# The last unit's ninth step sums the second buffer, and ScalarE centres the next batch's tokens: a fused attention and FFN kernel on one core

## The reference

```python
xn = layernorm(layernorm(x)) * g1 + b1         # queries: twice normalised
cn = layernorm(context) * g2 + b2
q, k, v = xn @ Wq.T, cn @ Wk.T, cn @ Wv.T      # 16 heads of 32
s = where(mask, q @ k.T / sqrt(32), -inf)      # [16 heads, 1024, 2048]
x1 = x + (softmax(s) @ v) @ Wo.T + bo
xd, wd = mx_fp6(layernorm(x1)), mx_fp6(W)      # blocks of 32 share a scale
out = x1 + xd @ wd.T + bias
```

## Time and profile before

| | |
|---|---|
| Median of 3 runs | 4500.66 us (4495.67 to 4505.8) |
| The profiled execution's own time | 4507.71 us |
| Its span | 4505.9 us |
| PE busy | 4345.9 us (96%) |
| DVE busy | 3443.6 us (76%) |
| ACT busy | 2814.4 us (62%) |
| POOL busy | 2718.9 us (60%) |
| Mean granted TensorE clock | 0.993 |
| Queue q0 (merges) | 318.79 MB, 35.3% of 16 engines' span |
| Queue q1 (loads and stores of SP) | 207.83 MB, 15.0% |

### The profile page before, as it was taken

One profiled execution on the slowest core, in us unless ns is written; L12 is line 12 of the kernel. 1 busy time (PEld: TensorE's weight loads), 2 busy tenths in 40 slices (PEclk: granted clock), 3 DMA queues, 4 the chain that ended last, 5 costly groups with the idle time before them and its releaser, 6 DMA issues.

```text
span 4505.9 us, 89640 instructions
## 1 busy us (share of the span) xinstructions
PE 4345.9 (96%) x36880; PEld 1506.5 (33%) x36880; DVE 3443.6 (76%) x4023; ACT 2814.4 (62%) x5128; POOL 2718.9 (60%) x1706
## 2 busy tenths in 40 slices
PE   4999999999999999999999999999999999999999
PEld 2322343223432234322343223422234222342223
DVE  5788667886678866888668886688866888668885
ACT  3387734877447864478645785458754587546784
POOL 2288552885428854388544885348853588525884
PEclk9999999999999999999999999999999999999999
DMA  5355642557326573356633556335663365543654
GB/s 191 73 118 118 150 136 61 120 118 180 109 59 123 114 192 99 68 117 121 177 100 69 119 120 175 102 77 116 123 167 106 75 123 115 167 111 74 123 113 108
DMA packets 190012, 532.35 MB, mean 118 GB/s; under 512 B 28625, under 2 KB 102673, under 8 KB 148386
## 3 DMA queue, kind: packets, MB, share of 16 engines
q0 software_dynamic: 43776, 318.79, 35.3%
q1 hardware_dynamic: 145826, 207.83, 15.0%
HBM read 110.98 MB, written 21.01 MB: 29 GB/s over the span
## 4 chain that ended last, share of the span: by engine, by line
PE 73%; DVE 12%; DMA 5%; ACT 4%; issue 3%; POOL 2%; SPq 0%; DVEq 0%; ACTq 0%; POOLq 0%
PE banks L1048 20%; PE banks L1060 17%; PE banks L956 16%; PE banks L1016 12%; PE banks L1091 5%; DVE max_parts L621 5%; DMA wdT<-wkT_wvT_wqT 3%; ACT region L835 2%; PE banks L925 2%; DMA sums<-wkT_wvT_wqT 2%; PE banks L950 1%; DVE amax L569 1%; DVE x_stats L536 1%; DVE region L759 1%; DVE qscale L571 1%
## 5 line engine op out<-in xcount | busy, mean ns | idle before, releaser
L621 DVE TENSOR_REDUCE max_parts<-banks 128x2 f32<-128x1024 f32 x2048 | 2402.1, 1218 | 454.3 <-PE banks L1016 442.4
L835 ACT ACTIVATE region<-banks 128x512 f32<-128x512 f32 x4096 | 2191.1, 616 | 506.2 <-PE banks L1048 401.1
L427 POOL TENSOR_TENSOR wkT_wvT_wqT<-region 128x1024 f32<-128x1024 f32 x528 | 1284.7, 2518 | 668.0 <-ACT region L835 662.6
L1048 PE MATMUL banks<-queries_stacked,keys_stacked 98*32 98x512 f16 x16384 | 1317.7, 384 | 21.6 <-ACT values L822 7.1
L1060 PE MATMUL banks<-region,values 128*32 128x512 f32 x8192 | 1076.8, 600 | 12.3 <-ACT region L835 9.2
L1048 PEld LDWEIGHTS banks<-queries_stacked,keys_stacked 98*32 98x32 f16 x16384 | 415.5, 95 | 1149.3 <-ACT region L835 842.0
L1016 PE MATMUL banks<-keys_stacked,queries_stacked 33*128 33x512 f16 x4096 | 701.5, 386 | 7.2 <-DVE max_parts L621 3.5
L956 PE MATMUL banks<-region,wkT_wvT_wqT 128*128 128x512 f16 x2304 | 557.3, 381 | 12.6 <-DMA wkT_wvT_wqT<-weights_split 10.3
L427 POOL TENSOR_TENSOR sums<-region 128x1024 f32<-128x1024 f32 x144 | 358.8, 2617 | 92.1 <-ACT region L835 91.8
L956 PE MATMUL banks<-wkT_wvT_wqT,region 128*128 128x512 f16 x1536 | 368.8, 380 | 0.0
L1016 PEld LDWEIGHTS banks<-keys_stacked,queries_stacked 33*128 33x128 f16 x4096 | 180.2, 93 | 559.4 <-issue 352.2
(11 more groups left out here) (92 smaller groups left out, 3224.0 us busy)
## 6 DMA issues: line engine op xcount, KB each, us to landing
wdT<-wkT_wvT_wqT POOLq DMA_DIRECT2D x96, 1024.0 KB, 11.7
wkT_wvT_wqT<-wkT_wvT_wqT POOLq DMA_DIRECT2D x80, 1024.0 KB, 7.3
sums<-wkT_wvT_wqT POOLq DMA_DIRECT2D x72, 1024.0 KB, 7.3
wkT_wvT_wqT<-sums POOLq DMA_DIRECT2D x40, 1024.0 KB, 7.2
region<-in_x SPq DMA_DIRECT2D x24, 1024.0 KB, 8.9
wkT_wvT_wqT<-weights_split SPq DMA_DIRECT2D x8, 3072.0 KB, 19.0
keys_stacked<-region SPq DMA_DIRECT2D x384, 64.0 KB, 2.0
keys_stacked<-sums SPq DMA_DIRECT2D x384, 64.0 KB, 2.0
```

What stands on the lines that cost most here:

```text
L427: e.tensor_tensor(SUMS[dst][:, half], PR[i][:, half], PR[i + 1][:, half], ALU.add).then_inc(s_pr, 1)
L621: e.tensor_reduce(mpart[:, buf, :, a, t, c], MXB[parity], AX.X, ALU.max).then_inc(s_mxd, 1)
L835: e.activation(PR[u % 4][:, j * HALF:j * HALF + HALF], score_bank(m % NU, kt, j)[0], ACT.Exp, scale=SCALE).then_inc(s_ex, 1)
L1048: mm = e.matmul(dst[HD * t:HD * t + HD, :], KA[0:STR, ds(ka + (j * C + (u + 1) * P + HD * t), HD)], QA[0:STR, ds(qa[j], HALF)], start=True ...
```

## The change

Five things are changed.

1. In unit 7, PE sums the second buffer of unit 6 in the ninth step (t = 8) and not in the sixth (t = 5). ACT copies the bank LB after it, in the tenth tile instead of the seventh.
2. In unit 7, DVE puts pair 4 and the adds of tiles 10 to 13 into the buffer one instead of second. That buffer is free once the unit's first merge has landed, and DVE waits for this. Pair 4 now comes ahead of the inverse of unit 6, and the wait for six steps of PE falls away.
3. SP loads the FFN weights right after the ninth step, ahead of the halves of x.
4. The centring of the next batch's query tokens goes from DVE to ACT, with a new shift made by POOL (`next_rstd`, three small instructions instead of one): chunk 0 at ACT's i = 4 and 5, two 128 x 512 activations each, and chunk 1, four of them, after ACT's last stage.
5. DVE takes chunk 1's statistics at i = 9, all at once, and not at i = 5 and 6.

```diff
-    NEXT_AT = (2, 6)
+    NEXT_AT = (2, T // P - 1)
...
+                e.wait_ge(s_pv, b * (NU * KT) + (NU - 1) * KT + 9 + 4)
+                e.dma_start(SUMS[4], wd_dram).then_inc(s_fl, 16)
...
                 e.wait_ge(s_pv, b * (NU * KT) + NU * KT + 4)
-                e.dma_start(SUMS[4], wd_dram).then_inc(s_fl, 16)
...
+                def next_rstd(c):
+                    e.wait_ge(s_ve, call_next(b, NEXT_AT[c]))
+                    e.wait_ge(s_nx, (b + 1) * NCH + c)
+                    e.tensor_tensor(rs[:, :], ve[:, :], mhalf[:, :], ALU.pow).then_inc(s_nr, 1)
+                    e.wait_ge(s_nr, 2 * (b * XCH + c) + 1)
+                    e.tensor_tensor(nb[:, :], mv[:, :, 0], rs[:, :], ALU.mult).then_inc(s_nr, 1)
+                    e.wait_ge(s_nr, 2 * (b * XCH + c) + 2)
+                    e.tensor_scalar(nb[:, :], nb[:, :], -1.0, None, ALU.mult).then_inc(s_rs, 1)
...
-                    if i in NEXT_AT and b + 1 < B:
-                        rstd(call_next(b, i))
+                    if i == NEXT_AT[0] and b + 1 < B:
+                        next_rstd(0)
                 if b + 1 < B:
-                    low_tokens(b + 1, 0, TF_FIRST)
+                    low_tokens(b + 1, 0, TF_FIRST, halfway=lambda: next_rstd(1))
...
-                                ins = e.tensor_tensor(SUMS[second][:, half], SUMS[second][:, half], PR[t % 4][:, half],
+                                ins = e.tensor_tensor(SUMS[one][:, half], SUMS[one][:, half], PR[t % 4][:, half],
...
                         pair(3, three)
+                        e.wait_ge(s_acc, (3 * m + 1) * 16)
+                        pair(4, one)
                         invert_first(m - 1)
                         invert_rest()
                         normalise(m - 1, n - 1)
-                        e.wait_ge(s_pv, m * KT + 4 + 6)
-                        pair(4, second)
...
-                parts = queries_tokens(b + 1, [call_next(b, i) for i in NEXT_AT]) if b + 1 < B else iter(())
+                parts = [token_stats(c, b + 1, call_next(b, NEXT_AT[c])) if b + 1 < B else iter(()) for c in range(XCH)]
...
+                    if i == TT + 1:
+                        for _ in parts[1]:
+                            pass
                     if i >= 3:
                         y_tile(i - 3)
-                    if i >= 1:
-                        next(parts, None)
+                    if 1 <= i <= NEXT_AT[0]:
+                        next(parts[0], None)
...
+                def centred(c, first, n):
+                    e.wait_ge(s_rs, call_next(b, NEXT_AT[c]))
+                    for i in range(first, first + n):
+                        ins = e.activation(chunk_tokens(c)[:, i, :], chunk_tokens(c)[:, i, :], ACT.Identity,
+                                           bias=nb[:, i:i + 1], scale=rs[:, i:i + 1])
...
-                            if kt == 7 and n > 0:
+                            if kt == 7 and 0 < n < NU - 1:
                                 halfway = lambda: row_sums(m - 1, KT + 6)
+                            if kt == 10 and end:
+                                halfway = lambda: row_sums(m - 1, KT + 9)
...
+                    if i in (4, 5) and b + 1 < B:
+                        centred(0, (i - 4) * 2, 2)
...
+                if b + 1 < B:
+                    centred(1, 0, 4)
...
+                    closing = 8 if end else 5
...
-                                if t == 5:
+                                if t == closing:
                                     sums = [(SUMS[4], (s_ac2, 16 * (b * (2 * NU - 2) + 2 * (2 * g + q))))]
```

More of the change, by code:

```diff
@@ L152, in build @@
             for n, w in (("mean_var", 2), ("var_eps", 1), ("rstd", 1), ("minus_mean_rstd", 1)))
+        nb = sb("minus_mean_rstd", [P, 4], F32)
         mhalf = sb("minus_half", [P, 4], F32)
@@ L208, in build @@
         s_rs = sem("rstd_ready")
+        s_nr = sem("next_rstd_made")
         s_nx = sem("tokens_normalised")
@@ L405, in _, with low_tokens @@
             for b in range(0, B):
-                def low_tokens(b, c, full, call=None):
+                def next_rstd(c):
[6 more added lines that the diff above has]
+                    e.tensor_scalar(nb[:, :], nb[:, :], -1.0, None, ALU.mult).then_inc(s_rs, 1)
+                def low_tokens(b, c, full, call=None, halfway=None):
                     for cc in range(CC):
@@ L412, in low_tokens @@
                             rstd(call)
+                        if cc == 1 and halfway:
+                            halfway()
                 if b == 0:
@@ L551, in centre, with token_stats @@
                 return e.tensor_scalar(dst, src, mean, rstd, ALU.subtract, ALU.mult)
+            def token_stats(c, b, call):
+                e.wait_ge(s_x[c % 3], b * (NCH // 3 * 16) + c // 3 * 16 + 16)
+                if c >= XCH:
+                    e.wait_ge(s_rs, call - 1)
+                yield from norm_stats([chunk_tokens(c)[:, i, :] for i in range(4)], stats, mv, ve[:, :], c < XCH)
             def norm(c, b, call):
@@ L555, in norm @@
                 twice = c < XCH
-                e.wait_ge(s_x[c % 3], b * (NCH // 3 * 16) + c // 3 * 16 + 16)
-                yield from norm_stats(tiles, stats, mv, ve[:, :], twice)
+                yield from token_stats(c, b, call)
                 yield
@@ L812, in turned @@
                                          scale=affine[:, 2 * x_side, cc:cc + 1]).then_inc(done, 1)
+                def centred(c, first, n):
[3 more added lines that the diff above has]
+                                           bias=nb[:, i:i + 1], scale=rs[:, i:i + 1])
+                    if first + n == 4:
+                        ins.then_inc(s_nx, 1)
                 def high_part(f, i, j):
@@ L1133, in quad @@
                                     sums = [(SUMS[buffers(2 * g + q - 1)[0]], (s_acc, 48 * m))]
-                                if t == 5:
+                                if t == closing:
                                     sums = [(SUMS[4], (s_ac2, 16 * (b * (2 * NU - 2) + 2 * (2 * g + q))))]
-                            step(m, n, ex, ka, qa, v, u, t + 1, rows[u], sums=sums, closing=t == 5,
+                            step(m, n, ex, ka, qa, v, u, t + 1, rows[u], sums=sums, closing=t == closing,
                                  between=(lambda: turn_next(ex)) if t == 9 and not end else None)
@@ L1153, in unit @@
                     if end:
-                        left = [(PR[3], None), (second, (s_pr, m * 14 + 16)), (first, (s_acc, 48 * (m + 1)))]
+                        left = [(PR[3], None), (one, (s_pr, m * 14 + 16)), (first, (s_acc, 48 * (m + 1)))]
                     else:
```

## The result

The changed kernel takes 4521.55 us, median of 10 runs (4515.26 to 4526.68), beside 4505.41 us of the kernel before, 10 runs too (4495.67 to 4509.35). The ratio is 1.0039, 95% interval 1.003 to 1.0048. It is slower by about 17 us, outside the range 4484 to 4514, and near the 4522 of the rival *Slower*. The prediction was put on the median of three runs of the kernel before, 4500.66; with ten runs that median is 4505.41, so 4.8 us of the distance to 4500 come from the starting point and some 17 from the sum.

What follows compares the result with a forecast made beforehand. PE was busy nearly all the time, with waits for `wdT` (11.2 us) and a chain of three merges in unit 7. Unit -6.8, load +9.6, clock +10.4, last stage -13.0 gave +0.2 us: 4500 us, range 4484 to 4514.

Steps and rivals of the forecast that it cites:

- Slower: Rival, chance 0.23: the merge waits for all of the load, 2.6 us, and the clock falls every batch; +21.8 us, 4522.
- The wait for the second buffer: Unit 7: PE's wait for `wdT` goes, but the third merge limits the gain to 0.85 us a batch, 6.8 in all.
- DVE's new order: Unit 7: DVE's later pair 4, inverse and adds stay hidden, PE ready 1.3 us ahead of the third merge; cost nothing.
- The load: FFN weights' load between second and third merge in unit 7: costs 1.2 us a batch, +9.6; bounds 0 and 2.6 us.
- The clock: PE's wait before unit 7's last sum lowers the clock in half of the batches: 4 x 2.6 = +10.4 us, bounds 0 and 20.8.
- The last stage: Batches one to seven: first to eighth tile takes the eighth batch's 45.4 us; -13.0 us over seven batches.
- The likeliest case: The wait only moves to PE's last sum, and the last stage pays for load and clock: 4500 us, chance 0.42.
- The clock holds: Rival, chance 0.15: the load costs 1.2 us, but PE's idle time is spread by other waits; -10.2 us, 4490.
- The load slips in: Rival, chance 0.20: the merge takes its turn, 0.3 us a batch, and the clock falls once; -14.8 us, 4486.

Runs made afterwards that it cites:

- the late load: Changed kernel with the FFN weights loaded at their old place, after the halves of x: 4481.73 us, ratio 0.9943 to the kernel before; repeated, 4481.9 us, 0.9932.
- the sooner half of x: Changed kernel with the FFN weights loaded at their old place and the first half of x issued as soon as tile 12 is added: 4484.93 us.
- The fill: Changed kernel with four unread products on PE ahead of its wait for the third merge in unit 7: 4508.19 us, ratio 1.0003 to the kernel before.
- the centring alone: Kernel before with only the centring moved to ACT and the late statistics, unit 7 and FFN weights' load as before: 4495.64 us, ratio 0.9974.
- the load two steps later: Changed kernel with the early load of the FFN weights issued two steps later: 4495.66 us, ratio 0.9975 to the kernel before.
- unit 7 alone: Kernel before with only the change in unit 7, centring left on DVE, FFN weights loaded at their old place: 4499.86 us, ratio 0.9991.
- half the load early: Changed kernel with half of the FFN weights (0.5 MB) loaded early, the other half at the old place: 4498.33 us, one run.

## Why the prediction was wrong, point by point

**The wait for the second buffer** went away as forecast, and its gain was cut by the third merge as forecast. Without the early load unit 7 is 7.8 and 8.4 us shorter in the two profiles with the late load (295.0 against 287.2 and 286.6), for a forecast of 6.8. That this is so close is partly luck: the sum had the last sum 31.0 us after that of first and the first tile 5.0 later, and the profile has 30.1 and 5.8. The merges are quicker than forecast (7.9 and 7.4 us, not 8.3 and 8.2), and x comes later against them, which the forecast had at nothing, or 0.5 us if the merge ends early.

**DVE's new order** was put at nothing. No step of PE in unit 7 waits for DVE, before the last sum or at it. ACT makes PE wait 0.4 to 1.1 us in most batches, 24 to 26 us after the sum of first; in the changed kernel this is hidden by the merge, as forecast. In the kernel with the late load PE has no wait for the merge in four of eight batches, and there it is no longer hidden.

**The load** is the step that failed. The mechanism was named, that the load stands ahead of the merge in a chain without slack, but the term of 1.2 us a batch was far too small. The second to third merge takes 2.75 us more with the early load than without (10.65 against 7.90), which is a little over the upper bound of 2.6; against the kernel before (8.34) it takes 2.3 more. Two things were wrong in how the term was worked out. The rate was taken from a stretch with many loads in flight, 2.6 us for 1 MB; this load takes 3.9 to 6.4 us, 5.0 in the mean. And the cost was taken to be the overlap of two stretches of time, but the merge also moves its own data more slowly behind the load. In the third batch the second to third merge takes 12.25 us, and 8.14 in the same batch with the late load: 4.1 us for this load alone. The load also costs at the third merge: it comes so late that the halves of x are queued behind it before its data is through, and it takes 8.3 us to PE's last sum and not the 7.4 of the kernel with the late load. The run with the sooner half of x shows the same from the other side, 8.0. The prediction had this in its 8.2, so it is no part of the miss. Against the late load the last sum is 3.5 us later in each batch, 28 us, where the prediction priced the load at 9.6. Against the prediction's own sum, which had 32.2 us with the load, it is 33.6: 1.15 us from the second merge, and 0.1 each from its issue and from the third.

**The clock** was taken to fall in half of the batches, 10.4 us. It fell in seven of eight, after waits of 4.1 us in the mean and not 2.5; in the fifth batch it held after 2.64. The first tile came 7.0 us after the last sum and not 5.0, which is 16.3 us over eight batches. The fill shows the clock's price by itself, 13 to 16 us. The clock's miss follows from the load's. Together the two make the unit 2.1 us a batch longer than forecast, 17 us, and with 1.3 us elsewhere that is nearly the whole way from the forecast +0.2 to the measured 18.9.

**The last stage** gave 13.0 us in the profile for 13.0 forecast, and 12 in the run with the centring alone. The eighth batch was the right measure for it. What was forecast of POOL and ACT (covered by some 1 us) was measured as 0.97 and 1.36 us.

**The numbers around the sum.** The likeliest case's own range was given as 4492 to 4509, "by the clock in two to six batches". Two clock losses fewer or more are 5.2 us either way, 4496 to 4506.

**The rivals.** *Slower* came true: the load served first and the clock lost nearly every time. Its last sum, 31.0 + 2.6 = 33.6 us after that of first, is what was measured, and so is PE's wait, 4.1 for 3.9. Its 4522 is closer to the 4521.55 than it deserves: it forecast 21.8 us more than before, and the profiles have 18.9 and the medians 16.1; the rest is the starting point, 4.8 us too low. *The clock holds* is out, with seven slow sums of eight. *The load slips in* is out, with a second to third merge of 10.65 us. It had drawn on a rule of the Trainium skill (DMA: Bandwidth & Descriptors, queues, rings and completion order), that the DMA engines take the queues in turn by whole packets. The prediction took the packet in hand to be a small part of the load. The same page says that 1 MB to 128 partitions is eight data descriptors for each engine (descriptor swizzle section, for a transfer issued by POOL) and a packet 9 to 17, so one packet could be the whole load. Read so, the rule would give what the third batch shows, no packet of the merge while most of the load runs, and what the load two steps later shows, none of the load while the merge runs. That is an inference and not shown. The profile counts 100 packets for 0.77 MB of the load, some 8 KB each; if these were the packets of the rule, a merge would get its turn after each of them, and in this stretch it did not.

What stays open: the centring alone gave 0.26% and unit 7 alone 0.09%, but both together 0.57 and 0.68%. The profiles of the four kernels don't show this excess: in unit and last stage the parts add up to 25 us, and the two kernels with both have 20.5 and 21.4. But the profiled executions of the two parts were the fastest runs of their kernels, and the medians are slower. The granted clock of all runs explains a part. In the 57 runs of the kernel before that stood beside the experiments, the time goes with the mean granted clock, from 4516 us at 0.991 to 4500 at 0.996, some 3 us for each 0.001. Against the kernel before beside it, the centring alone has 0.002 more, unit 7 alone 0.001, and both together 0.004 and 0.005. By that slope, which is an estimate, the clock makes 2 to 5 us of an excess of 9 to 12. The rest was not traced.

## What to carry to other kernels

A load that is moved to an earlier, seemingly idle moment must be checked against the DMA chain that ends last: issued just ahead of a link of that chain, the load made the link wait, 2.75 us in the mean for 1 MB, and issued some 4 us later it cost a third of that. A wait that PE sits out near the end of a stage can cost a second time, when the clock falls behind it; here four products that nobody needs won that part back. And a member of a loop that has less to do than the others, here the eighth batch, shows what the others gain when they are freed of that work.

## What the runs showed that was not expected

- A load that was served as soon as it was issued, right ahead of a merge, moved 0.77 MB in 3.5 us (0.22 MB/us) and took 3.9 to 6.4 us for its 1 MB in the eight batches; the same load, queued for 3.4 us behind a merge, moved 1.03 MB in 3 us (0.34) and took 3.1 to 4.4.
- With a row of 2 KB for all 128 partitions ahead of it, a load of x landed 2 us later (7.6 us after its issue, not 5.6), though the row is a quarter of a MB.
- A load queued behind a merge, before that merge is through, makes its landing later by 0.6 to 0.8 us in the mean, though the merge's data is ahead.
- After waits of 2.9 us the granted clock fell in one batch and held in another: in the kernel with half the load early the last sum took 1.93 us after a wait of 2.91, and 1.06 after one of 2.86.
